# Second attention's identity products moved, second experts' ReLU ahead of the sum and transposes two experts ahead

## What is computed

```
# second attention, one head; k = v = ctx_1024, q = layernorm(x)
scores = (q Wq + bq) (ctx Wk)^T / 16
x = x + softmax(scores) (ctx Wv + bv) Wo + bo

# second experts, on xr = layernorm(x), 1792 rows
gate = softmax(xr @ Wg); idx = argmax(gate)      # one expert for each row
h = relu(dispatched @ w1)                        # each expert: at most 112 rows, 256 -> 1024
expert_out = h @ w2                              # 1024 -> 256
x = x + expert_out[idx] * gate[idx]              # rows over the limit of an expert add nothing
```

## Time and profile before

| | |
|---|---|
| median of three runs | 772.79 us (769.84 to 773.85) |
| profiled execution | 771.14 us, span 769.3 us |
| TensorE busy | 720.3 us, 94% of the span |
| VectorE, ScalarE, GpSimd busy | 419.7, 325.5, 218.0 us |
| mean granted TensorE clock | 0.971 |
| DMA | 128.12 MB, mean 167 GB/s |

### The profile page before, as it was taken

The page is one execution under the profiler, slowest core; times in us unless marked ns, Lnnn a source line. Parts: engine busy times, 40 slices in busy tenths (PEclk is TensorE's granted clock), DMA queues, the critical chain, the costliest instruction groups (busy, mean ns, idle before and its releaser), DMA issues. The chain is left out here.

```text
span 769.3 us, 19472 instructions
## 1 busy us (share of the span) xinstructions
PE 720.3 (94%) x6739; PEld 569.3 (74%) x6740; DVE 419.7 (55%) x1269; ACT 325.5 (42%) x884; POOL 218.0 (28%) x359
## 2 busy tenths in 40 slices
PE   5789999999999999999997898998999989999995
PEld 4457667777667776667665698997788878999994
DVE  4556877778877778776763322222588861111111
ACT  1335665555665556655553143331455540110110
POOL 3212333313333213243110023333356531111111
PEclk8979999999999999999999799999999998999998
DMA  6737554345653446642535459853566633999950
GB/s 173 197 98 195 139 144 107 91 126 166 173 150 103 126 139 174 170 124 74 177 117 156 123 184 259 212 171 104 168 202 217 198 105 111 309 327 342 332 160 17
DMA packets 99527, 128.12 MB, mean 167 GB/s; under 512 B 23394, under 2 KB 84683, under 8 KB 99312
## 3 DMA queue, kind: packets, MB, share of 16 engines
q1 hardware_dynamic: 90193, 115.07, 51.2%
q0 software_dynamic: 3824, 8.46, 3.6%
q10 hardware_dynamic: 5423, 3.48, 1.9%
HBM read 74.68 MB, written 23.88 MB: 128 GB/s over the span
## 5 line engine op out<-in xcount | busy, mean ns | idle before, releaser
L564 ACT ACTIVATE probs<-psum 128x448 f32<-128x448 f32 (+2 forms) x256 | 125.2, 541 | 57.9 <-PE psum L917 57.4
L776 DVE TENSOR_REDUCE neg_max<-psum 112x2 f32<-112x750 f32 x128 | 118.7, 928 | 6.5 <-PE psum L900 4.7
L900 PE MATMUL psum<-stacks 96*128 96x487 bf16 (+1 forms) x256 | 75.5, 377 | 4.6 <-DVE neg_max L777 2.6
L917 PE MATMUL psum<-stacks 102*128 102x112 bf16 (+1 forms) x1024 | 76.9, 214 | 1.6 <-ACT probs L564 0.4
L932 PEld LDWEIGHTS psum<-probs,rings 128*32 128x32 f32 (+2 forms) x2048 | 44.9, 109 | 45.2 <-issue 36.8
L917 PEld LDWEIGHTS psum<-stacks 102*128 102x128 bf16 (+1 forms) x1024 | 54.4, 98 | 30.4 <-ACT probs L564 23.8
L932 PE MATMUL psum<-probs,rings 128*32 128x112 f32 (+2 forms) x2048 | 75.8, 265 | 0.0
L1954 DVE SCALAR_TENSOR_TENSOR e_y<-psum,e_x_in 112x256 f32<-112x256 f32 x16 | 7.7, 484 | 98.0 <-PE psum L2002 98.0
L1988 PEld LDWEIGHTS psum<-e_xt,rings 128*128 128x128 f32 x512 | 59.5, 192 | 2.2 <-ACT e_xt L1934 1.3
L1988 PE MATMUL psum<-e_xt,rings 128*128 128x112 f32 x512 | 59.7, 275 | 0.9 <-ACT e_xt L1934 0.9
L2002 PE MATMUL psum<-rings,e_hid 128*112 128x256 f32 x256 | 57.9, 379 | 1.3 <-DVE e_hid L1961 1.3
(11 more groups left out here) (228 smaller groups left out, 1392.3 us busy)
## 6 DMA issues: line engine op xcount, KB each, us to landing
rings<-in_L_ffn_w SPq DMA_DIRECT2D x32, 1024.0 KB, 7.7
stacks<-rings SPq DMA_DIRECT2D x96, 243.5 KB
ct_dram<-rings SPq DMA_DIRECT2D x16, 375.0 KB, 4.9
a_ct<-ct_dram SPq DMA_DIRECT2D x16, 375.0 KB, 4.4
a_ctx<-in_ctx SPq DMA_DIRECT2D x16, 375.0 KB
stacks<-q_parts SPq DMA_DIRECT2D x93, 56.0 KB
rings<-in_ctx SPq DMA_DIRECT2D x16, 256.0 KB
w<-in_L_ffn_W SPq DMA_DIRECT2D x8, 512.0 KB, 6.2
```

The source lines that it names most:

```text
L564: nc.scalar.activation(probs[k % 4][0:keys, :, :], src, ACT.Exp, scale=DH ** -0.5).then_inc(s["exp_done"], 1)
L776: nc.vector.tensor_reduce(neg_max[:, 0, h:h + 2], psum[0:T, pair:pair + 2, 0:S], AX, ALU.max, negate=True)
L900: last = nc.tensor.matmul(bank[2 - 2 * (k % 2) + j][0:rows, 0:KV], q_flat[n.third][0:QK, h * T:h * T + rows], k_stack[n.third][0:QK, h, :] ...
L917: last = nc.tensor.matmul(bank[4 + k % 2][0:wide, j * T:(j + 1) * T], k_flat[n.third][:, first:first + wide], q_stack[n.third][:, h, :], s ...
```

## The change

In the second attention, the identity products stand elsewhere: seven new ones ahead of the transposes of the last batch (step 18), none any more ahead of the counts in step 18, three instead of four in step 19.

In the second experts, VectorE's step does the ReLU of `e - 1` first and the sum of `e - 2` second. On TensorE, experts 0 and 1 are both transposed ahead of step 0, and step `e` transposes `e + 2` instead of `e + 1`, at the same place between up of `e` and down of `e - 1`; the loop ends accordingly earlier. SP, ScalarE and GpSimd have the same program as before.

```diff
                     if (b - 3).real():
                         n = b - 3
+                        if n.c == B - 1:
+                            g.keep_busy(bank[0], 7)
                         pe.wait_ge(s["xn3"], n.count(1, 1))
...
                             pe.wait_ge(s["q"], b.count(2, 2))
-                        elif b.c > B + 1:
-                            g.keep_busy(bank[0], 4)
+                        elif b.c == B + 3:
+                            g.keep_busy(bank[0], 3)
                         r.count(pe, b - 4)
...
             def _(dve):
                 def step(e):
+                    if (e - 1).real():
+                        n = e - 1
+                        dve.wait_ge(s["up"], n.count(2, 2))
+                        if (n - 2).real():
+                            dve.wait_ge(s["down"], (n - 2).count(1, 1))
+                        nc.vector.tensor_scalar(hid[n.parity][:, KF // 2:KF, :], bank[2 * n.parity + 1][:, 0:4 * C1].rearrange("p (f t) -> p f t", f=KF // 2),
+                                                0.0, None, ALU.max).then_inc(s["hid_v"], 1)
                     if (e - 2).real():
                         n = e - 2
                         dve.wait_ge(s["down"], n.count(1, 1))
...
-                    if (e - 1).real():
-                        n = e - 1
-                        dve.wait_ge(s["up"], n.count(2, 2))
...
                 transpose_in(Item(0, 0, E1, 4))
+                transpose_in(Item(0, 1, E1, 4))
...
-                    if (e + 1).real():
-                        transpose_in(e + 1)
+                    if (e + 2).real():
+                        transpose_in(e + 2)
...
-                steps(pe, step, E1, 3, E1 - 2, E1 + 1, 4)
+                steps(pe, step, E1, 3, E1 - 3, E1 + 1, 4)
```

## The result

The changed kernel takes 845.4 us in the median of six runs (843.7 to 851.7), the kernel before 772.4 us: a ratio of 1.097, 95% interval 1.093 to 1.1005. The forecast was 831 us with a range of 803 to 848.

The account below looks back on a forecast made before the run. The second experts run at TensorE's pace, with DMA engines having just enough room. 771.1 - 1.5 (tail) + 1.9 (start) + 38.4 (rows) + 22.8 (clock) - 1.3 (ReLU) = 831.4, so 831 us, range 803 to 848.

Parts of the forecast that it names:

- The rows come late: Second experts: rows land after transposes two ahead want them; twelve waits of 3.2 us, experts 4 to 15, +38.4 us.
- the ring: Second experts: each down ends later, so the next rows are issued later by as much; the wait isn't paid off.
- The start of the stage: Second experts' start: copies save 0.4 us, transposes wait 2.3 us for rows of expert 3; +1.9 us.
- The clock: TensorE in second experts: low clock after each of 13 waits, 1.75 us each; +22.8 us, bounds 0 and twice that.
- Rival B's first variant: Second experts: low-clock stretches last twice as long, half of the second under up; 843 us, chance 0.13 for both variants.
- rival A: TensorE in second experts: the clock holds through the waits, all else equal; 808.6 us, chance 0.21.
- The attention's tail: Second attention's last batches: moved identity products shorten VectorE's waits for counts; -1.5 us, bounds 2.65 gain and 1.75 loss.
- The ReLU: VectorE in second experts: ReLU ahead of the sum delays nothing, removes the last down's 1.31 us wait; -1.3 us.
- B: Second experts, deeper loss: longer low-clock stretches, or rows landing only after 7.7 us; 843 to 860 us, chance 0.13.
- B's second variant: SP's queue keeps its backlog, rows take 7.7 us; 28 us more, 859 us, chance 0.13 for both variants.
- C: SP's queue: rows served beside the weights, landing before transposes want them; not slower, 768 us, chance 0.05.
- The sum: Whole kernel: profiled time plus all terms gives 831.4, taken as 831 us; own range 818 to 842, chance 0.61.

Follow-up runs that it names:

- the last version: Kernel before with ReLU ahead of the sum, identity products moved (25 at phase end), expert 1 transposed ahead of step 0, others one ahead: 765.6 us, ratio 0.9941.

## Why the prediction was right, and where it was off

**The rows come late: right.** Thirteen waits, forecast 13; their place, their releaser and the ring in which each delays the next are as forecast. Undoing the one edit, doing it alone, and the two ways of bringing the rows in time all say the same. Of the price, twelve waits of 3.2 us were forecast and 42.4 were measured (44.6 less the first, 2.13): 3.5 each. The step that was small is the landing: 6.0 us in the median, where I took 5.1 to 5.9 from the earlier trace rows. The DMA rate fell to 172 GB/s between the first and the last wait; about 190 was forecast.

**The start of the stage: half right.** The wait for the rows of expert 3 was put at 2.3 us and was 2.13. For the copies 0.4 us were forecast; both waits for them are gone from the list, 0.9 us together. Not foreseen there was the first up at the low clock, 6.56 us instead of 3.83: +2.7. The prediction had named that gap at the barrier as a bound of the attention's part, at 1.75.

**The clock: right mechanism, wrong size.** This is the mis-sized term. I forecast 13 x 1.75 = 22.8 us and took the price from one gap of 2.15 us; the busy time of the stage says 38.5. Less the first up, that is 35.8 over 13 waits, 2.75 us each. The profile of the transposes alone gives 2.4. The first two waits behaved as the prediction had it: the clock was 1.00 through the wait and fell behind it, and the downs took 5.19 and 5.31 us, 1.6 and 1.7 more than at full clock. From the third wait on the clock fell while TensorE still waited (0.78 to 0.84 over the wait), the transposes were slow too, and the downs took 5.9 to 6.3 us. The length of the wait doesn't tell the two kinds apart, as the second and the twelfth wait of the changed kernel show:

```profile
670.22 0.41 PE L1975 MATMUL psum<-ident,e_x_in 112*128 112x112 f32 x2 [3.27 <-DMA e_x_in<-sorted]
670.47 5.31 PE L2005 MATMUL psum<-rings,e_hid 128*112 128x256 f32 x16
...
805.83 0.64 PE L1975 MATMUL psum<-ident,e_x_in 112*128 112x112 f32 x2 [3.24 <-DMA e_x_in<-sorted]
806.26 6.25 PE L2005 MATMUL psum<-rings,e_hid 128*112 128x256 f32 x16
```

What does is open. Rival B's first variant, 843 us, had longer low stretches, but laid half of what they add under up, which has cover; here up ran at full clock (3.72 us) and the low stretch lay on the wait, the transposes and the down. With the clock kept by filled waits the time was 817.7 us, above rival A's 808.6, whose waits were too short by 0.4 each.

**The attention's tail: right, slightly small.** 2.0 us were gained where 1.5 were forecast, both waits for counts being nearly gone; in the changed kernel's profiled execution the first up gave them back.

**The ReLU: right in the profile.** The wait of 1.31 us is gone; in the time alone it can't be shown.

**The rivals.** By the time alone the forecast and B (843 to 860) can't be told apart: 845.4 lies just inside B. The profile decides against B's second variant: the rows land after 6.0 us and not 7.7, the waits are 3.5 us and not 5.5. C, not slower, fell on what it rested on: the rows did stand behind the weights. The experiment that put them ahead came to a landing of 2.9 us and 778 us, near the 774.5 that the prediction gave for 2.7 us. The estimate of 2.5 us for one transfer, from the Trainium skill's page "DMA: Bandwidth & Descriptors" (section "Anatomy of one DMA — SWDGE (gpsimd) path"), fits those loads: 2.6 us at the least, 2.9 in the median. It doesn't fit loads that queue behind a megabyte (6.0 us). That section of the Trainium skill gives its price for transfers that GpSimd issues; SP issues these.

**The sum.** 831 forecast, 845.4 measured: inside the range that took in the rivals, outside the forecast's own 818 to 842. The clock (+15.7 in the profiled execution) and the waits (+4.0) were small. That execution lies 6 us above the median and had the lowest mean granted clock of the six (0.921; the others 0.925 to 0.939), so the clock's part in the median should be a few us less; no profile shows it.

## What to carry to other kernels

Moving a step ahead moves every wait inside it ahead; ask first when its data can arrive, and count from the event that frees the buffer, not from the usual landing time. Where an engine takes its work in the order of the code, as TensorE does in these timelines, a wait put in front of ready work delays all of it, and here a wait that recurred in each turn of a ring was never caught up. Where a small load decides and large ones only prefetch, issue the small one first (778.4 us here), or issue it a turn earlier into more buffers (767.2 us, with two more).

## What the runs showed of the hardware

The waits of TensorE cost nearly as much again in clock: in the changed kernel 42.4 us more of idle time brought 38.5 us more of busy time for the same products, 2.7 of them in the first up behind the barrier; with the transposes alone, 45.4 us of waits for rows came with 31.8. In the changed kernel the clock fell in every turn with waits of 2.1 to 4.1 us; with the transposes alone it stayed at 1.00 after one wait of 3.39 us in thirteen. With the waits filled, gaps of up to 1.6 us left it at 1.00 throughout the stage. A gap of 1.7 us at the barrier was followed by a low first up in the changed kernel, one of 1.1 us in the last version was not. Products whose results nobody reads, put where the time was lost anyway, took 27.7 us off.
